# Scatters of edge weights given out anew over the blocks of an eight-stage graph network kernel

## The reference, cut to what matters

```python
edge_index = jnp.stack([src, dst])
x = x + _L0_gnn_ref(_layernorm(x), ..., src, dst)           # mean over neighbours, two products
x = x + _L0_ffn_ref(_layernorm(x)[None], ...)[0]            # top half of the tokens, gelu FFN
x = x + _L1_gnn_ref(_layernorm(x), ..., edge_attr_3, edge_index)  # graph attention, 8 heads
x = x + _L1_ffn_ref(_layernorm(x)[None], ...)[0]            # top 1 of 8 experts
x = x + _L2_gnn_ref(_layernorm(x), src, dst, edge_weight, ...)
x = x + _L2_ffn_ref(_layernorm(x)[None], ...)[0]            # top 2 of 8 experts
x = x + _L3_gnn_ref(_layernorm(x), ..., edge_index)         # two normalised graph convolutions
x = x + _L3_ffn_ref(_layernorm(x)[None], ...)[0]
```

```python
h = x @ weight_l
msgs = edge_val[:, None] * h[edge_col]
agg = jax.ops.segment_sum(msgs, edge_row, num_segments=N)
out = agg + bias_l + x @ weight_r + bias_r
```

## Time and profile before

| | |
|---|---|
| median of 3 runs | 3462.41 us (3462.06 to 3463.84) |
| the profiled execution | 3466.76 us, span 3465.0 us |
| mean granted TensorE clock | 0.933 |
| busy, share of the span: PE, PEld | 2931.3 us (85%), 2144.0 us (62%) |
| busy: DVE, ACT, POOL | 2045.2 us (59%), 1156.7 us (33%), 2040.5 us (59%) |
| 416 scatters of weights (L162) on POOL | 458.9 us, 1103 ns each |
| 416 scatters of counts (L153) on POOL | 411.7 us, 990 ns each |
| 416 gathers of the sum of edges (L535) on POOL | 415.9 us, 1000 ns each |

### The profile page before, as it was taken

One profiled execution on the slowest core, in us unless ns is written; L12 is line 12 of the kernel. 1 busy time (PEld: TensorE's weight loads), 2 busy tenths in 40 slices (PEclk: granted clock), 3 DMA queues, 4 the chain that ended last, 5 costly groups with the idle time before them and its releaser, 6 DMA issues. The chain is left out here.

```text
span 3465.0 us, 49010 instructions
## 1 busy us (share of the span) xinstructions
PE 2931.3 (85%) x15083; PEld 2144.0 (62%) x15109; DVE 2045.2 (59%) x4851; ACT 1156.7 (33%) x2529; POOL 2040.5 (59%) x2061
## 2 busy tenths in 40 slices
PE   4888888897899999619996897999949979898788
PEld 3666667686455555309894565555729955456677
DVE  7666666984688888899997245200254444214432
ACT  4555553332222222229993221100123321103210
POOL 5777775776677777676555776477766723000064
PEclk9999999998899999859998899999969989999989
DMA  5555554102799989836662432645052254435253
GB/s 192 185 183 183 186 184 137 48 1 68 210 264 264 264 263 259 275 140 197 197 197 86 134 114 96 238 149 157 10 166 62 68 189 161 150 109 198 112 173 108
DMA packets 286321, 552.64 MB, mean 159 GB/s; under 512 B 63009, under 2 KB 181734, under 8 KB 285558
## 3 DMA queue, kind: packets, MB, share of 16 engines
q1 hardware_dynamic: 203238, 390.67, 34.0%
q0 software_dynamic: 82832, 158.84, 16.6%
HBM read 375.63 MB, written 174.69 MB: 159 GB/s over the span
## 5 line engine op out<-in xcount | busy, mean ns | idle before, releaser
L162 POOL DMA_INDIRECT edge_weights<-shares,share_cell x416 | 458.9, 1103 | 220.6 <-PE bank L1575 117.7
L153 POOL DMA_INDIRECT edge_counts<-repeats,count_cell x416 | 411.7, 990 | 137.3 <-issue 116.9
L535 POOL DMA_INDIRECT layer_gnn_sum_rows<-xn_rows,src_cols x416 | 415.9, 1000 | 126.6 <-issue 112.3
L1249 POOL DMA_INDIRECT layer_gnn_s_rows<-gat_rows,src_cols x416 | 402.3, 967 | 148.1 <-issue 117.5
L1297 PE MATMUL bank<-layer_gnn_h_nodes,layer_gnn_s_onehot_t 128*128 x1664 | 485.4, 415 | 0.9 <-DVE layer_gnn_s_onehot_t L1318 0.2
L599 PE MATMUL bank<-layer_gnn_sum_onehot,layer_gnn_sum_rows 128*128 128x256 f32 x832 | 275.5, 415 | 86.8 <-DMA layer_gnn_sum_rows<-xn_rows,src_cols 76.8
L1297 PEld LDWEIGHTS bank<-layer_gnn_h_nodes,layer_gnn_s_onehot_t 128*128 128x128 f32 x1664 | 283.8, 190 | 79.8 <-issue 4.3
L1307 ACT ACTIVATE layer_gnn_s_enc<-bank 128x256 f32<-128x256 f32 x416 | 159.4, 383 | 414.4 <-PE bank L1290 406.5
L2844 PE MATMUL bank<-layer_gnn_b_weights,xn_nodes 128*128 128x391 f32 x768 | 255.1, 494 | 28.6 <-DMA layer_gnn_b_weights<-edge_weights 28.6
L1574 PE MATMUL bank<-layer_gnn_w_onehot,layer_gnn_w_part 128*128 128x256 f32 x832 | 250.8, 383 | 12.8 <-DVE layer_gnn_w_part L1619 12.2
L736 DVE TENSOR_TENSOR edge_sums_turned<-edge_sums_turned,bank 128x512 f32 x208 | 142.9, 687 | 160.4 <-PE bank L600 157.0
(11 more groups left out here) (651 smaller groups left out, 6142.4 us busy)
## 6 DMA issues: line engine op xcount, KB each, us to landing
kept_rows<-layer_gnn_s_rows SPq DMA_DIRECT2D x104, 512.0 KB, 4.1
layer_gnn_w_rows<-kept_rows SPq DMA_DIRECT2D x104, 512.0 KB, 4.4
edge_weights<-layer_gnn_sum_zeros SPq DMA_DIRECT2D x108, 400.0 KB
layer_gnn_b_weights<-edge_weights SPq DMA_DIRECT2D x54, 782.0 KB, 4.8
layer_gnn_gcn_sum_counts<-edge_counts SPq DMA_DIRECT2D x50, 836.0 KB, 4.5
layer_gnn_s_dst_across<-in_dst_row SPq DMA_DIRECT2D x104, 256.0 KB
edge_counts<-layer_gnn_no_edges SPq DMA_DIRECT2D x25, 836.0 KB, 8.4
layer_ffn_e_w<-in_l1f_w SPq DMA_DIRECT2D x16, 1024.0 KB
```

What stands on the lines that cost most here:

```text
L153: nc.gpsimd.indirect_dma_start(g.counts, bass.IndirectOffsetOnAxis(ap=g.cell[:, sent(t):sent(t) + 1].bitcast(U32), axis=0), g.repeats[:, s ...
L162: nc.gpsimd.indirect_dma_start(g.weights, bass.IndirectOffsetOnAxis(ap=g.share_cell[:, sent(t):sent(t) + 1].bitcast(U32), axis=0), g.share ...
L535: nc.gpsimd.indirect_dma_start(rows[:, t % U, :], None, table, bass.IndirectOffsetOnAxis(ap=g.srcc[:, t:t + 1].bitcast(U32), axis=0)).then ...
L1249: nc.gpsimd.indirect_dma_start(rows[:, t % U, :], None, htable, bass.IndirectOffsetOnAxis(ap=g.srcc[:, t:t + 1].bitcast(U32), axis=0)).the ...
```

## The change

The two tuples get other values and a constant SOON = 13 is new, so the same 832 scatters go out in other places. The iota goes from the sum of edges into the loading block, behind POOL's last work there, and writes `g.shares`, which is free until the sum's end; VectorE reads it from there into `own`.

| weight scatters | before | after |
|---|---|---|
| beside the neighbours' product (new program on POOL) | 0 | 13 |
| start of the first FFN | 20 | 20 |
| beside its hidden layer | 118 | 108 |
| attention's features | 36 | 20 |
| softmax | 36 | 24 |
| beside the weighted sum | 148 | 190 |
| gate and routing of the second FFN | 16 + 16 | 16 + 16 |
| its first two experts | 13 + 13 | 4 + 5 |

| count scatters | before | after |
|---|---|---|
| second FFN's experts | 97 | 112 |
| products of the third graph layer | 239 | 224 |
| gate, routing of the third FFN | 12, 26 | 12, 22 |
| its experts | 42 | 46 |

```diff
--- before.py
+++ after.py
@@ -79,7 +79,7 @@
         x_cleared, idx_loaded = sem("x_cleared"), sem("idx_loaded")
         g.x_cuts = (0, 6, LN_FIRST, FULL)
         g.x_in = [sem(f"x_in{k}") for k in range(3)]
-        consts, ident0, win = sem("consts"), sem("ident_cleared"), sem("win_ready")
+        consts, ident0, win, numbered = sem("consts"), sem("ident_cleared"), sem("win_ready"), sem("own_numbered")
         win_sum, step = sem("win_sum"), sem("window_step")
         wi = stack.enter_context(nc.sbuf_tensor(g.tag + "window_tile", [1, ET], I32))
         df = stack.enter_context(nc.sbuf_tensor(g.tag + "dst_f", [P, ET], F32))
@@ -106,6 +106,8 @@
             pool.wait_ge(ident0, 1)
             nc.gpsimd.affine_select(out=g.ident[:, :], in_=g.ident[:, :], compare_op=ALU.not_equal, fill=1.0,
                                     base=0, pattern=[[-1, P]], channel_multiplier=1).then_inc(consts, 1)
+            nc.gpsimd.iota(g.shares[:, :], [[1, GROUPS], [0, 2]], base=NODES, channel_multiplier=0, allow_small_or_imprecise_dtypes=True).then_inc(numbered, 1)
+            pool.wait_ge(numbered, 1)
 
         @block.vector
         def _(dve):
@@ -478,8 +480,8 @@
         gathered = [sem(f"gathered{u}") for u in range(U)]
         key_in = [sem(f"key_in{k}") for k in range(2)]
         zeroed, weights_in, shared = sem("weights_zeroed"), sem("weights_in"), sem("shared")
-        cleared, negated, far, hot, summed, added, rows_in_, row_key, stored, step, numbered, last_seen, lined, spread, ones_cast = (sem(n) for n in (
-            "cleared", "negated", "far", "hot", "tile_summed", "tile_added", "rows_in", "row_key", "stored", "step", "numbered", "last_seen", "lined", "spread", "ones_cast"))
+        cleared, negated, far, hot, summed, added, rows_in_, row_key, stored, step, last_seen, lined, spread, ones_cast = (sem(n) for n in (
+            "cleared", "negated", "far", "hot", "tile_summed", "tile_added", "rows_in", "row_key", "stored", "step", "last_seen", "lined", "spread", "ones_cast"))
         matched, counted, turned, lifted, product, used, done = (sem(n) for n in (
             "matched", "counted", "turned", "lifted", "product", "used", "done"))
         zeros = sb("zeros", [P, SRC // 4])
@@ -528,7 +530,6 @@
 
         @block.gpsimd
         def _(pool):
-            nc.gpsimd.iota(own[:, :], [[1, GROUPS], [0, 2]], base=NODES, channel_multiplier=0, allow_small_or_imprecise_dtypes=True).then_inc(numbered, 1)
             for t in range(ET):
                 if t >= U:
                     pool.wait_ge(summed, (t - U) // 2 + 1)
@@ -658,8 +659,7 @@
             in_groups = lambda v: v.rearrange("p (q k) -> p q k", k=2)
             nc.vector.tensor_tensor(in_groups(low[:, 2:ET]), in_groups(dstf[:, 2:ET]),
                                     in_groups(g.ps[7][:, 0:ET - 2])[:, :, 1:2].to_broadcast([P, GROUPS - 1, 2]), ALU.is_equal).then_inc(step, 1)
-            dve.wait_ge(numbered, 1)
-            nc.vector.tensor_tensor(own[:, :], own[:, :], dstf[:, :], ALU.subtract).then_inc(step, 1)
+            nc.vector.tensor_tensor(own[:, :], g.shares[:, :], dstf[:, :], ALU.subtract).then_inc(step, 1)
             dve.wait_ge(step, 10)
             nc.vector.tensor_tensor(own[:, :], own[:, :], low[:, :], ALU.mult).then_inc(step, 1)
             nc.vector.tensor_copy(high[:, :], high_i[:, :]).then_inc(step, 1)
@@ -744,11 +744,18 @@
             dve.wait_ge(shared, 2 * NG0)
 
 
+SOON = 13
+
+
 def layer0_neighbours(nc, g, w_neigh, inv):
 
     with ExitStack() as stack:
         product, added = nc.alloc_semaphore(g.tag + "nb_product"), nc.alloc_semaphore(g.tag + "nb_added")
         block = stack.enter_context(nc.Block(g.tag + "neighbours"))
+
+        @block.gpsimd
+        def _(pool):
+            place_weights(nc, g, pool, 0, SOON)
 
         @block.tensor
         def _(pe):
@@ -842,8 +849,8 @@
         self.nc.vector.tensor_copy(self.xnt[:, :, t * P:(t + 1) * P], self.bank(t).rearrange("p (c n) -> p c n", c=2)).then_inc(self.placed, 1)
 
 
-PLACED = (20, 138, 174, 210, 358, 374, 390)
-COUNTED = (97, 302, 336, 348, 374)
+PLACED = (33, 141, 161, 185, 375, 391, 407)
+COUNTED = (112, 300, 336, 348, 370)
 KEEP = max(1, int(0.5 * NODES)) - 1
 H0 = 1024
 NEG = -3.0e38
@@ -880,7 +887,7 @@
                 nc.gpsimd.affine_select(out=before[:, :], in_=g.ones[:, :], compare_op=ALU.is_gt, fill=0.0, base=0,
                                         pattern=[[-1, P]], channel_multiplier=1).then_inc(passed, 1)
 
-                place_weights(nc, g, pool, 0, PLACED[0])
+                place_weights(nc, g, pool, SOON, PLACED[0])
                 for t in range(0, NT):
                     front.normed(pool, t)
                     nc.gpsimd.tensor_tensor(g.x[:, t, :], g.x[:, t, :], g.xn[:, t, :], ALU.add).then_inc(passed, 1)
```

## The result

The changed kernel's median over six runs is 3446.65 us (3442.72 to 3447.34); the kernel before had 3464.08 in its six runs (3462.06 to 3468.33). The ratio is 0.9943, 95% interval 0.9933 to 0.9953: faster by 0.57%, or 19.7 us of 3464.1, with 16.3 and 23.2 as the interval's ends. The two medians themselves are 17.4 us apart. The forecast was 3440.5, a ratio of 0.9937, with 3434 to 3452 as the range.

What follows compares the result with a forecast made beforehand. A block begins only when every engine has left the one before, so block ends bound the kernel. Terms of −2.5 − 1.3 − 12.0 − 2.4 − 1.0 − 2.9 + 0.2 = −21.9 us gave median 3440.5, range 3434 to 3452.

Steps and rivals of the forecast that it cites:

- The two prices of a block's end: Between blocks: next block follows soon after ScalarE, VectorE or SP ends last, but 3.2 us after a POOL scatter.
- the features: Attention's features: 20 scatters for 36 let SP's landing set the block's end; −12.0 us, bounds −13.0 and −9.4.
- The rival of the smaller gap: Features' end: another engine holds it at 867, so the term is −9; chance 0.13.
- First FFN, products, routing: Ends of first FFN, third layer's products, second routing: fewer scatters let POOL finish sooner; −1.3, −1.0, −2.9 us.
- The weighted sum: Weighted sum: 190 scatters for 148 over 208 pairs cost nothing, pair stays 1.31 us; 0, bounds 0 and +3.
- The rival of the held pairs: Weighted sum: added scatters hold VectorE's pairs, at 0.96 us each +18.4 us overall, 3480.8; chance 0.05.
- Landings clog: Weighted sum and last experts: POOL's scatters wait for landings; the change ends between 3446 and 3462; chance 0.08.
- TensorE's clock: After the features: clock returns sooner, saving up to half of 9.1 busy us more, 3436.0; chance 0.09.
- 13 beside the neighbours' product: Neighbours' product: 13 scatters fit in POOL's 33.88 us of idle, with 2.3 us of landing waits; cost 0.
- The iota: Sum of edges: iota moved into loading block starts POOL's gathers 2.6 us earlier; −2.5 us, bounds −1.3 and −3.9.
- The second FFN's experts: Second FFN's experts: two fewer scatters bring POOL to the last expert's puts earlier; −2.4 us, bounds 0 and −2.6.
- The last experts: Third FFN's experts: 46 counts for 42, where POOL just keeps up with TensorE; +0.2 us, bounds 0 and +5.1.

Runs made afterwards that it cites:

- 28 scatters: Changed kernel with 28 scatters in the attention's features in place of 20, softmax 16 in place of 24; median 3450.22 us, ratio 0.9951.
- the 44 left out: Changed kernel with 44 of 416 weight scatters omitted, leaving 146 beside the weighted sum in place of 190; median 3449.15 us, ratio 0.9951.
- the features alone: Kernel before with only 16 of the features' 36 scatters moved beside the weighted sum; median 3455.35 us against 3467.38, ratio 0.9963.

## Why the prediction was right, and where it wasn't

The time, 3446.65, lies in the range, and the sign and the cause are those forecast; the median came out 6 above the forecast, the profile's span 21.3 below before where −21.9 was summed. That the profile agrees so closely is in part luck: the terms of the two experts' stages were wrong by 3.3 and 2.3 us, and the stages where the sum had 0 gave 4.1 us in all (the neighbours' product alone 1.7, by the clock), which no edit can be shown to have earned.

*The two prices of a block's end, and with them the features.* Right. −12.2 and, alone, −11.9; 28 scatters brought the crossing within 0.5 us of where the sum has it. The rival of the smaller gap falls. The price of 3.2 us holds at the ends that a scatter sets in the first FFN, the features and the products (2.8 to 3.7), but it is not a constant, as the weighted sum shows.

*First FFN, products, routing.* Right in mechanism, −1.6, −1.4 and −2.4 for −1.3, −1.0 and −2.9. In the routing the next block follows VectorE's end by 1.14 us where I had put 0.35. Over all profiles the routing is 45.7 to 46.8 us in the three with 26 counts and 43.3 to 43.9 with 22, so its term holds at 3.0.

*The weighted sum.* Right: 42 more cost nothing, by the 44 left out about 0.01 us each. The rival of the held pairs falls, and with it the Trainium skill's rule (page "SBUF — State Buffer", section "Who interferes with whom") as a price for this kernel: VectorE's L1626 with its two SBUF inputs is not held by the scatters. That an indirect transfer issued by POOL counts as an instruction that reads SBUF was the prediction's own reading of that rule. "Landings clog" did not come at 190: 6.3 us of waits for landings, all of them within POOL's slack. But the margin was smaller than my sum had it. I had put 3.2 us behind POOL's last scatter; its queue's drain alone took 6.59, and ended 3.28 us before VectorE. The limit, between 200 and 208 scatters, lies where that tail and the last scatter pass VectorE's end, and not in a price of each scatter, where I had looked for it.

*TensorE's clock.* This rival did not come in the changed kernel's profile, but my reading of it was off. I had let the fall stand at 866; it came 8.5 us earlier, at 856.6 for 865.1. The lower level then lasted to 873.7, 17.1 us and not 27.3, yet TensorE was busy for 9.4 us in it, as before, so nothing was won, and the 0.9 us of scores and softmax are within their scatter. In two other profiles it did come: with the features alone and with 28 scatters there, the lower level ended 11.0 and 10.9 us after the edge scores' first instruction, for 15.5 in the changed kernel, 16.3 before and 12.6 to 16.3 over all the other twelve, and scores and softmax took 669.3 and 669.6 us for 670.6 to 673.5. That is 1 to 2 us of the 4.5 that I had put for it; what decides it was not tried.

*13 beside the neighbours' product.* Cost 0, as forecast; no wait for a landing came at all there, where 2.3 us had been put. The 1.7 us gained in the profile are the clock's chance, which I had not in the sum.

*The iota.* −2.5 is not shown. −3.1 in the first pair of profiles, but the stage scatters by 7.8 us from profile to profile, and three comparisons don't separate the move from nothing. The mechanism's near side is seen, the first gather 1.8 us nearer the block's begin; whether it reaches the end is open.

*The second FFN's experts.* Wrong, and this is the step that failed: "POOL arrives 2 × 1.28 = 2.6 earlier, at 2143.6 or before, since scatters that waited for landings also go". Two transfers fewer were right, but waits for landings did not go, they grew from 3.4 us to 7.7, and the stage was 0.9 us longer and not 2.4 shorter (261.8 to 263.8 us in the eight profiles with 112 counts, mean 263.0; 262.6 to 263.0 in the three as before, mean 262.7). What is sure is that the 2.4 didn't come; that the stage got longer is not. The bound of 0 for that term was too near as well. Two transfers' worth against two waits' worth is a difference of small numbers on a list of 187 indirect transfers, and I had priced only one of them. With 15 counts fewer the gain came, 2.5 us.

*The last experts.* Mis-sized: +0.2 was forecast, +2.5 seen. Over the profiles the stretch is 234.2 to 236.6 us in the nine with 46 counts (mean 235.0) and 233.5 to 234.9 in the five with 42 (mean 234.4), so most of the 2.5 is chance and the counts cost about 0.6. Of that 0.33 us is seen: POOL's drain at this block's end takes 7.30 to 7.31 us behind the last transfer in the nine profiles with 46 counts and 6.97 to 6.99 in the five with 42.

*The median.* The ratio says −19.7, interval −16.3 to −23.2, the profile −21.3. In the second session the same kernel gave −13.9 (−9.0 to −18.7). The sum of −21.9, less 2.5 for the iota and 3.3 for the experts, would be −16.1, between the two.

## What to carry to other kernels

Where blocks begin only when all engines are done, read each block's end: which engine is last, what its last instruction adds behind itself (about 3 us behind a scatter in most blocks here, 9.4 where 208 had gone before it, 0.3 to 1.6 behind the other engines), and who is last without it. Moving background transfers pays only at those ends, by the distance to the second engine, and not by their number. On a list that is full, price the waits along with the instructions: where a place has room for one in 1.31 us and one takes 1.26, fill it to nine in ten, not to one for each step, and look at the queue's drain as well as at the last instruction: 200 of 208 were free with 0.27 us to spare. And repeat a profile before reading a stage's change of 1 or 2 us as the edit's doing.

## What the runs showed of the hardware that was not expected

The same stage with the same instructions took 24.5 or 26.2 us (neighbours' product, 14 profiles: five at 24.5, nine at 26.2, none between), with TensorE's granted clock 1.00 or 0.94 over it: a stretch of 3.4 us at the lower level at its begin, or none. No edit chose which. The sum of edges, 416 indirect gathers in a row, took 548.7 to 556.5 us. With one scatter for each pair in the weighted sum, the next block began 9.36 us after POOL's last scatter, where at the other ends that a scatter sets it was 2.8 to 3.7. The drain of POOL's queue there took 2.99, 3.16, 4.46, 6.59, 7.40 and 8.06 us behind the last scatter with 146, 148, 164, 190, 200 and 208 of them in the block.
